# Other starting places in SBUF for the split weights of a gated two-layer kernel

## The reference

```python
# x (2, 1024, 256)
x = x + (einsum('bsd,bdh->bsh', x, W[cat_ids]) + b[cat_ids][:, None, :])

def _dense(x, wi, wo):                      # wi (256, 1024), wo (1024, 256)
    return relu(x @ wi) @ wo
s0 = _dense(x, swi[0], swo[0])
s1 = _dense(x, swi[1], swo[1])
eo = relu(x @ wi[type_label]) @ wo[type_label]      # one expert for each sequence
gate_in = concatenate([eo[:, 0], s0[:, 0], s1[:, 0]], axis=-1)
w = softmax(relu(gate_in @ g1) @ g2)
x = x + eo * w[0] + s0 * w[1] + s1 * w[2]
```

## Time and profile before

| | us |
|---|---|
| median of 3 runs | 271.71 |
| lowest and highest | 271.42 and 271.82 |
| the profiled execution | 271.66 |
| its span, first to last instruction | 269.8 |

### The profile page before, as it was taken

How to read it: one execution, slowest core, us unless ns; L and a number is a source line. 1 busy time by engine, 2 the same in 40 slices (tenths; PEclk the granted TensorE clock), 3 DMA queues, 4 the chain that set the end, 5 groups by cost and what they waited for, 6 DMA issues and landing times.

```text
span 269.8 us, 3491 instructions
## 1 busy us (share of the span) xinstructions
PE 265.1 (98%) x1182; PEld 220.3 (82%) x1182; DVE 160.9 (60%) x241; ACT 148.2 (55%) x257; POOL 160.8 (60%) x170
## 2 busy tenths in 40 slices
PE   8999999999999999999999999999999999999994
PEld 8788887888888888888888888888888888888884
DVE  3879958635644444654445565345566477685684
ACT  2597357665565655665655653745644555645320
POOL 0179989999948949938944724724725528524000
PEclk9999999999999999999999999999999999999999
DMA  6735322022012022102022112112012022000008
GB/s 193 247 106 155 117 78 79 7 75 79 6 74 78 6 73 78 58 24 78 2 78 78 34 46 78 33 46 79 19 61 78 2 78 75 2 0 2 0 12 299
DMA packets 7328, 18.30 MB, mean 68 GB/s; under 512 B 1168, under 2 KB 1936, under 8 KB 7312
## 3 DMA queue, kind: packets, MB, share of 16 engines
q1 hardware_dynamic: 6592, 16.92, 18.4%
q10 hardware_dynamic: 720, 1.18, 1.4%
HBM read 16.00 MB, written 2.10 MB: 67 GB/s over the span
## 4 chain that ended last, share of the span: by engine, by line
PE 96%; DMA 2%; SPq 1%; DVE 0%; issue 0%; ACT 0%; DVEq 0%
PE acc L657 48%; PE chain L657 24%; PE right L657 12%; PE left L657 7%; PE acc L674 4%; DMA w_raw<-cat_w 2%; PE corner L657 1%; SPq L222 1%; PE left L813 0%; DVE x L648 0%; ACT w_hi L352 0%; PE left L819 0%; SPq L224 0%; DVEq L647 0%
## 5 line engine op out<-in xcount | busy, mean ns | idle before, releaser
L264 POOL TENSOR_TENSOR m_lo<-staged,m_hi 128x512 fp32r<-128x512 f32 (+1 forms) x48 | 81.5, 1706 | 80.5 <-ACT m_hi L340 65.7
L657 PE MATMUL acc<-h_hi,m_hi 128*128 128x512 f32 x190 | 73.9, 389 | 0.0
L657 PE MATMUL acc<-h_hi,m_lo 128*128 128x512 f32 x190 | 73.9, 389 | 0.0
L657 PE MATMUL acc<-h_lo,m_hi 128*128 128x512 f32 x190 | 73.9, 389 | 0.0
L364 ACT COPY kept<-chain 128x512 f32<-128x512 f32 x66 | 38.8, 588 | 57.8 <-PE chain L657 57.8
L657 PEld LDWEIGHTS acc<-h_hi,m_lo 128*128 128x128 f32 x190 | 35.7, 188 | 7.4
L657 PEld LDWEIGHTS acc<-h_hi,m_hi 128*128 128x128 f32 x190 | 35.7, 188 | 7.4
L657 PEld LDWEIGHTS acc<-h_lo,m_hi 128*128 128x128 f32 x190 | 35.7, 188 | 7.4
L471 DVE SCALAR_TENSOR_TENSOR h_lo<-left,h_hi 128x512 fp32r<-128x512 f32 x24 | 16.6, 692 | 29.9 <-ACT h_hi L376 29.9
L264 POOL TENSOR_TENSOR staged<-staged 128x128 f32<-128x128 f32 x66 | 30.9, 482 | 1.7
L476 DVE TENSOR_TENSOR left<-left,kept 128x512 f32<-128x512 f32 x22 | 15.3, 698 | 26.7 <-PE left L657 26.7
(11 more groups left out here) (107 smaller groups left out, 442.7 us busy)
## 6 DMA issues: line engine op xcount, KB each, us to landing
staged<-mlp_w SPq DMA_DIRECT2D x22, 512.0 KB, 3.3
x<-x_t ACTq DMA_DIRECT2D x4, 256.0 KB, 3.9
staged<-mlp_w SPq DMA_DIRECT2D x4, 256.0 KB, 3.3
x<-x_t SPq DMA_DIRECT2D x4, 256.0 KB, 5.4
out_t<-x SPq DMA_DIRECT2D x2, 512.0 KB, 3.3
g_sb<-g SPq DMA_DIRECT2D x1, 768.0 KB, 3.8
out_t<-x SPq DMA_DIRECT2D x3, 256.0 KB, 3.0
w_raw<-cat_w SPq DMA_DIRECT2D x4, 128.0 KB, 3.1
```

What stands on the lines that cost most here:

```text
L264: return nc.gpsimd.tensor_tensor(out, a, b, ALU.subtract)
L657: last = nc.tensor.matmul(out[:, columns], half[:, slot, at:at + P], moving[:, columns], start=(start and n == 0), stop=(stop and n == 2), ...
```

## The change

The rows of m_hi get 48 more columns for each slot (192 bytes), those of m_lo 16 more (64 bytes), which nobody reads or writes. Two spacers, 120 columns between m_hi and m_lo and 72 behind m_lo, are added. Nothing else differs.

```diff
 PAD = 40
+SHIFT_HI, BETWEEN, SHIFT_LO, BEHIND = 48, 120, 16, 72
...
-        m_hi = sb("m_hi", [P, SLOTS, SPLIT], F32R)
-        m_lo = sb("m_lo", [P, SLOTS, SPLIT], F32R)
+
+        m_hi = sb("m_hi", [P, SLOTS, SPLIT + SHIFT_HI], F32R)
+        sb("between", [P, BETWEEN])
+        m_lo = sb("m_lo", [P, SLOTS, SPLIT + SHIFT_LO], F32R)
+        sb("behind", [P, BEHIND])
```

## The result

The changed kernel takes **277.24 us** (median of 4 runs, 277.15 to 277.40) against 271.62 us for the kernel before on the same chip: ratio 1.0205, 95% interval 1.0192 to 1.0217. It is 2% slower, +5.6 us. The forecast was 271.7 us, no change; the measured time is just inside its range, on the side of the rival.

A forecast was written before the change was run, and what follows sets the result against it. TensorE, busy 98% of a 269.8 us span, was taken as the bound, a count of matmuls times a step; 850 × 0 + 290 × 0 + 0 for the writers = 0 gave 271.7 us, range 266.0 to 277.4 us.

The forecast's parts named there:

- the rival: Slower by the reads: weight loads at new distances hold the matmuls beside them; +3.7 us, 275.4 us, far end 283.0; chance 0.28.
- the value taken for an unseen distance: Cost of each matmul whose weights get a new distance from the moving part: taken as 0, 850 × 0.
- half of an extreme price on 850 matmuls: Range's upper end, 277.4 us: +5.7 us, half the far end of 850 × 13.3 = +11.3 us.
- Places that differ by whole multiples of 512 bytes make no difference: Layer 0, outputs and products, with different tensors and places, all step 226.7 ns; supported cost 0.
- The nine steps of 231 ns behind a stall: Nine starts from 47.53 to 49.61 us after a wait, 4.4 ns over the usual; priced dearer at 850 × 4.4 = +3.7 us.
- The count: 850 of 1140 matmuls change distance: 364 loading m_lo, 486 loading m_hi slots 1 and 2; 290 don't.
- The 384 bytes: New distance of m_hi slot 2 from the moving parts, taken as 128 short of the next 512.
- The writers: ScalarE's casts and GpSimd's subtractions on moved slots: cost 0, covered by idle time; as a rival 273.9 us, chance 0.02.
- the slower case: Reads at new distances lengthen steps; signs: matmuls above 0.39 us, three kinds of groups, m_lo steps unlike m_hi; chance 0.28.
- The 9 us: Estimate from the skill's page: some 10.8 ns unexplained per matmul, 9 us over 850 matmuls if new distances freed them.
- the 13.3 ns left over: Part of each matmul's step beyond its columns, with 256 and 512 columns; perhaps weight changing or the two reads meeting.
- the rival "distance 0 was the bad one": Two reads meet at equal places and now part: half freed −5.7 us, 266.0 us; all, 260.4 us; chance 0.19.

The follow-up runs named there:

- e6: Against the kernel before, all six slots of m_hi and m_lo placed 256 bytes behind the moving parts: 271.64 us, ratio 1.0006.
- e11: Against the kernel before, m_hi slots at 0, 256, 512 bytes and m_lo slots at 256, 512, 768 behind the moving parts: 271.61 us, ratio 0.9999.
- e8: Against the kernel before, weights stay; moving parts of outputs and layer 0 placed 32 bytes behind weights, products kept at distance 0: 277.45 us, ratio 1.0220.
- e12: Against the kernel before, slots of m_hi and m_lo at 0, 128 and 256 bytes, only slot 1 off a multiple of 256: 274.75 us, single run.
- e1: Against the kernel before, all six slots of m_hi and m_lo placed 32 bytes behind the moving parts: 278.35 us, ratio 1.0246.
- e7: Against the kernel before, all six slots of m_hi and m_lo placed 64 bytes behind the moving parts: 278.39 us, ratio 1.0252.
- e2: Against the kernel before, only m_hi moved (distances 0, 192, 384 bytes by slot), m_lo left at 0: 276.53 us, ratio 1.0179.
- e3: Against the kernel before, only m_lo moved (distances 32, 96, 160 bytes by slot), m_hi left at 0: 277.40 us, ratio 1.0212.
- e4: Against the kernel before, m_hi and m_lo of a slot both at 64, 128, 192 bytes for slots 0, 1, 2: 278.00 us, single run.

## Why the prediction was wrong

**The step that failed** is the value taken for an unseen distance. I took 0 because over a thousand steps in four kinds of moving part were equal. But every one of them had distance 0, as the same paragraph says: many rows at one value of a quantity say nothing of another value. In its place the runs show 5.5 ns on a mid-program step in the changed kernel, 6.7 ns at a steady 32 or 64 bytes, and 0 only at 256. That 277.24 us still lies inside the range is luck: its upper end, half of an extreme price on 850 matmuls, stands for 6.65 ns each and was not worked out from any distance. "Places that differ by whole multiples of 512 bytes make no difference" was right, and holds for 256 (e6, e11), but it was never the question.

**The right row was there**. The nine steps of 231 ns behind a stall come close to the changed kernel's mean of 232. Read with e8 and e12, they show that the 226.7 ns are a settled state that a disturbance breaks for about ten matmuls. I put them down as odd and priced the rival with them at +3.7 us, 275.4 us. They weren't the only ones either, as I had written. Before has two more such stretches: layer 0's first half takes 5.76 us where the second takes 5.44, and behind the gate's small matmuls at 215.5 us nine steps take 2.08 us again:

```profile
216.21 0.40 PE L657 MATMUL chain<-t_hi,m_lo 128*128 128x512 f32 x1
...
218.29 0.39 PE L657 MATMUL acc<-h_hi,m_lo 128*128 128x512 f32 x1
```

The same kind of stretch three times is a mechanism to be asked after, not an oddity.

**The size** of that rival was short for two reasons. The price of a step at a fixed distance is 6.7 ns (e1, e7), not 4.4; and the 242 matmuls of slot 0 that I had left out aren't spared. From the first product of group 2 to that of group 23 the changed kernel's trace takes 5.0 us more, the direct groups in front 0.2, group 0's outputs 0.15 and the last group 0.4; start and end of the two executions differ by 0.1 us the other way. Counted as 1092 matmuls (all but layer 0's) the 5.6 us are 5.1 ns each.

**The count** of 850 holds modulo 256 too, but it isn't what decides: 486 touched matmuls in e2 cost 4.8 us, 364 in e3 5.7 us, 363 in e12 3.1 us. It matters how good and bad ones alternate.

**The 384 bytes** of slot 2 I read as 128 short of 512. With a period of 256 they are simply a distance of 128.

**The writers** were right: same durations, no new wait in the chain, cost 0 (in mid-program the room is even 4.5 us for a pair of 3.5, more than the "nearly twice" that I wrote). Two signs of the slower case came, matmul records above 0.39 us and three kinds of groups. The third, m_lo matmuls that step otherwise than the m_hi ones, didn't: among the outputs all three steps of a product average 231.8 to 232.6 ns.

**The notes.** The steps of e1 against those of before show that two reads of TensorE do act on each other's time: 6.7 ns a matmul for a distance of 32 bytes. The Trainium skill (SBUF — State Buffer, Who interferes with whom) calls the two read ports independent; what I drew from that, that an address relation has nothing to act on, doesn't hold here, and the measurement decides. The 9 us that I had worked out from the Trainium skill's TensorE: Matmul & The Clock Gate (Wait — 56ns, not 53.3ns?) were not to be had: with 512 columns no run took anything from the 13.3 ns left over at distance 0. With 256 columns two did, and halved them (e7 and e4, 113.3 for 120 ns). So the rival "distance 0 was the bad one" was wrong for the time of this kernel and half right for its last twelve matmuls.

**What stays open**: what the two reads share. The runs show a period of 256 bytes and a rhythm with memory; that they meet in parts of the memory that repeat every 256 bytes is a reading that fits, and it was not measured by itself. It doesn't say either why 64 bytes cost 6.7 ns with 512 columns and give 6.7 ns back with 256. Which pair counts is open too, a matmul with its own weights or with the load that runs beside it: in e2 and e3 the two give different matmuls, but the cost spreads over all steps (in e3 they average 230.8 to 233.4 ns among the outputs). Nor is it known where the rest of the 13.3 ns comes from, or what starts a disturbance where TensorE doesn't wait. No version faster than the kernel before was found; 16, 32, 64, 128 and 256 bytes everywhere, and 96, 160 and 192 in mixtures, are covered.

## What to carry to other kernels

Where TensorE is the bound and each matmul brings its own weights, compute where weights and moving parts begin modulo 256 bytes. With 512 columns keep the two equal: here it is worth up to 2.4% of the time, and a spacer costs nothing. With 256 columns try other distances first, 64 bytes for one. Mixing good and bad places doesn't average, since a disturbance takes eight to ten matmuls to pass and one bad matmul in three (e3) keeps it up; so all of them have to be in line, and a check of the step from start to start (not of busy shares, 98% in both) shows whether they are. And when a trace holds only one value of what a change moves, its regularity is no evidence that the value doesn't matter.

## What the runs showed of the hardware that I had not expected

- A 128x512 float32r matmul with its weight load has a step of 226.7 ns when weights and moving part begin at equal places modulo 256 bytes, and 233.3 ns at distances of 32 and 64 bytes (232.4 ns at 128).
- With 256 columns it is 120 ns at equal places and 113.3 ns at 64 bytes (e7) and at 192 (e4).
- The distance counts and not the place: everything moved by 32 bytes together gives 271.64 us, the weights alone 278.35 us.
- The step has memory. At distance 0 it needs about eight to ten matmuls to settle again; at 16 bytes it stays at 226.7 ns up to 204 us and goes for whole groups at 233.3 ns behind that.
